# Count matrices of a graph kernel: bins added up in two strips in SBUF, each strip written once

## The reference, cut to what matters

```python
x, src, dst, edge_attr_64, edge_type_100 = inputs          # (3125,128), (103125,), (103125,), (103125,64), (103125,)
# layer 0: messages over edges with edge features
h = leaky_relu(concat([x[dst], edge_attr_64], axis=1) @ msg_w1 + msg_b1)
aggregated = segment_sum(h @ msg_w2 + msg_b2, src, num_segments=3125)
# layer 1: attention over edges; layer 2 and 3: normalised and plain mean of neighbours
alpha = exp(e - m[dst]) / denom[dst];  coef = rel_table[edge_type_100, 0] * alpha
out = segment_sum(coef[:, None] * z[src], dst, num_segments=3125)
```

## Time and profile before

| | us |
|---|---|
| median of three runs | 3433.16 |
| lowest, highest | 3431.87, 3433.22 |
| span of the profiled execution | 3432.5 |
| mean granted TensorE clock, share of full | 0.868 |
| DVE busy | 2686.0 (78%) |
| PE busy | 2529.2 (74%) |
| POOL busy | 1979.1 (58%) |
| ACT busy | 1648.7 (48%) |

### The profile page before, as it was taken

The page is one execution under the profiler, slowest core; times in us unless marked ns, Lnnn a source line. Parts: engine busy times, 40 slices in busy tenths (PEclk is TensorE's granted clock), DMA queues, the critical chain, the costliest instruction groups (busy, mean ns, idle before and its releaser), DMA issues. The chain is left out here.

```text
span 3432.5 us, 87712 instructions
## 1 busy us (share of the span) xinstructions
PE 2529.2 (74%) x20390; PEld 1959.9 (57%) x20391; DVE 2686.0 (78%) x8325; ACT 1648.7 (48%) x4130; POOL 1979.1 (58%) x2344
## 2 busy tenths in 40 slices
PE   2433555555555555999999999999999329989899
PEld 1322334443334434888888888888887214444454
DVE  8853777777777765999999999999997779993501
ACT  2011222222222224888888888888886655452200
POOL 1005777777777777888888888888887000000000
PEclk9976666677666677999999999999999559999999
DMA  9993222222222215888888888888887569868766
GB/s 382 412 414 117 79 78 78 78 78 83 78 77 78 78 63 145 230 227 229 230 227 228 231 225 228 231 227 230 228 227 244 215 284 352 300 235 304 250 218 203
DMA packets 738172, 696.85 MB, mean 203 GB/s; under 512 B 48523, under 2 KB 637274, under 8 KB 734778
## 3 DMA queue, kind: packets, MB, share of 16 engines
q1 hardware_dynamic: 516770, 536.77, 46.7%
q10 hardware_dynamic: 195544, 104.71, 12.6%
q0 software_dynamic: 25792, 54.52, 4.8%
HBM read 340.91 MB, written 354.90 MB: 203 GB/s over the span
## 5 line engine op out<-in xcount | busy, mean ns | idle before, releaser
L855 POOL DMA_INDIRECT sorted_rows<-rows,posi x806 | 784.1, 973 | 338.9 <-issue 316.6
L1137 DVE SCALAR_TENSOR_TENSOR acc<-acc,keep,pm 128x256 f32<-128x256 f32 x1504 | 717.4, 477 | 23.0 <-issue 8.3
L964 POOL TENSOR_SCALAR ohs_e<-iota,rt 128x128 f32<-128x128 f32 x1128 | 663.6, 603 | 12.5 <-DMA rt<-sorted_rows 12.5
L1064 PE MATMUL pm<-ohw_e,ohs_e 128*128 128x128 f32 x3008 | 662.6, 302 | 0.0
L803 PE MATMUL s_peq<-sb_w1bb,eT 128*128 128x256 f32 x806 | 352.2, 531 | 397.7 <-ACT eT L658 378.8
L973 POOL TENSOR_TENSOR hid<-pre_e,excess 128x512 f32<-128x512 f32 x376 | 511.8, 1361 | 141.6 <-ACT excess L1000 141.6
L1070 PE MATMUL px<-PN,dT 128*128 x4512 | 498.3, 219 | 0.1
L1016 ACT ACTIVATE ohw_e<-ohd_e,rt 128x128 f32<-128x128 bf16 x1504 | 474.6, 386 | 0.0
L1064 PEld LDWEIGHTS pm<-ohw_e,ohs_e 128*128 128x128 f32 x3008 | 459.4, 193 | 0.0
L803 PEld LDWEIGHTS s_peq<-sb_w1bb,eT 128*128 128x128 f32 x806 | 172.6, 264 | 439.4 <-ACT eT L658 431.1
L1081 PE MATMUL ps<-hid,ohs_e 128*128 128x129 f32 x3008 | 417.9, 281 | 1.2 <-POOL hid L973 1.1
(11 more groups left out here) (317 smaller groups left out, 4275.0 us busy)
## 6 DMA issues: line engine op xcount, KB each, us to landing
count_matrices<-acc SPq DMA_DIRECT2D x1504, 128.0 KB, 2.4
sorted_rows<-zrow SPq DMA_DIRECT2D x188, 528.0 KB, 10.1
rt<-sorted_rows ACTq DMA_DIRECT2D x184, 528.0 KB, 4.5
gab<-count_matrices SPq DMA_DIRECT2D x60, 1280.0 KB, 6.0
arb<-count_matrices SPq DMA_DIRECT2D x25, 1664.0 KB, 9.0
ab<-count_matrices SPq DMA_DIRECT2D x25, 1600.0 KB, 9.0
arb<-count_matrices SPq DMA_DIRECT2D x25, 1536.0 KB, 8.4
ef<-in_edge_attr_dram SPq DMA_DIRECT2D x58, 364.0 KB
```

The costliest lines, as they stand in the source:

```text
L855: pool.indirect_dma_start(sortd, bass.IndirectOffsetOnAxis(ap=posi[:, h, c:c + 1], axis=0), rows[:, h, c, :], None).then_inc(s_sc[h], 16)
L964: last = nc.gpsimd.tensor_scalar(ohs[:, k % BUFS, j, :], iota128[:], rt[:, k, j, D + 1:D + 2], None, ALU.is_equal)
L1064: last = nc.tensor.matmul(pm[:, q, j % 2, P:2 * P], ohs[:, kp % BUFS, j, :], ohw[:, kp % BUFS, j, :], start=True, stop=True)
L1137: nc.vector.scalar_tensor_tensor(acc[:, k % SUMS, j, :], before, keep[:, at:at + 1] if isinstance(at, int) else keep[:, ds(at, 1)], pm[:, ...
```

## The change

`acc`, `keep` and the table's row numbers go. In their place DVE holds two strips of 25 bins each in SBUF (`strips`, 128 x 2 x 51 x 128: two matrices, two slots of 25 columns of 128, and a blank column of zeros). A collect adds `pm` to the strip's column of its bin, or, for the first tile of a bin, to the blank column, and writes it into the bin's column. Which column is read and which is written stands in the table, and is loaded into registers: eight values a group and, by a load of its own with a check of its bounds, the strip's number, from which a wait on the writes (`s_w`) is computed. SP waits in each of 25 steps until `s_acc` has reached the tile count at which a strip ends (`ends`), and writes the strip in one transfer of 128 x 2 x 3200 numbers (3.28 MB). `ohw` and `dT` move into the space of `H`, which isn't in use in this stage. The operation of the collect is `tensor_tensor` in place of `scalar_tensor_tensor`. In the first stage one of three counting loops goes, and the transfer of `keep` to all partitions.

```diff
+SLOTS2 = 2
+BLANK = SLOTS2 * NT
-        tilei = msb("tilei", [1, 3, TT], I32)
-        keep = msb("keep", [P, TT])
+        tilei = msb("tilei", [2, 2, TT], I32)
+        ends = msb("ends", [1, NT], I32)
...
+                    nc.vector.tensor_copy(ends[:], incb[0:1, :].rearrange("p (s d) -> p s d", d=NT)[:, :, NT - 1])
-                    for k in range(3):
+                    for k in range(2):
                         for j in range(TCOL):
                             ins = nc.vector.tensor_scalar(junk4[:, j % 4, :], incb[:], kidx[:, k, j:j + 1], None, ALU.is_le,
                                                           ALU.add, accum_out=table[:, k, j:j + 1])
...
-                    act.dma_start(keep[:], tilef[0:TT].partition_broadcast(P)).then_inc(s_tl, 16)
-                    for k in range(3):
-                        act.dma_start(tilei[:, k, :], tiler[k:k + 1, 0:TT]).then_inc(s_tl, 16)
+                    for k in range(2):
+                        act.dma_start(tilei[k:k + 1, :, :], tiler[2 * k:2 * k + 2, 0:TT].unsqueeze(0)).then_inc(s_tl, 16)
...
-            acc = sb("acc", [P, SUMS, G, 2 * P])
+            strips = sb("strips", [P, 2, BLANK + 1, P])
...
             @block.sync
             def _(sp):
-                def step(i, k):
-                    n = i * RING + k
-                    rows = loads(nc, mybir.EngineType.SP, tilei[0:1, 2, ds(n * G, G)], DUMMY + SUMS * G - 1)
-                    for j in range(G):
-                        sp.wait_ge(s_acc, n * G + j + 1)
-                        sp.dma_start(ar[:, ds(rows[j], P, NT), :].rearrange("a p c -> p a c"),
-                                     acc[:, k % SUMS, j, :].rearrange("p (a c) -> p a c", a=2)).then_inc(s_w[k % SUMS], 16)
+                for s in range(NT):
+                    o = s % SLOTS2 * NT
+                    done = sp.value_load(ends[0:1, s:s + 1], min_val=1, max_val=TT)
+                    if s:
+                        sp.wait_ge(s_w, 16 * s + 32)
+                    sp.wait_ge(s_acc, done)
+                    sp.dma_start(strip[s], strips[:, :, o:o + NT, :].rearrange("p a q c -> p a (q c)")).then_inc(s_w, 16)
...
-                nc.vector.memset(acc[:], 0.0)
+                nc.vector.memset(strips[:, :, BLANK:BLANK + 1, :], 0.0)
+                nc.vector.memset(strips[:, :, 0:1, :], 0.0)
...
-                def collect(i, k, first, j):
+                def collect(i, k, first, j, at):
                     n = i * RING + k
                     if j % 2 == 0:
                         dve.wait_ge(s_m, 2 * n + j // 2 + 1)
-                    if j == 0 and not (first and k < SUMS):
-                        dve.wait_ge(s_w[k % SUMS], (i * (RING // SUMS) + k // SUMS) * (16 * G))
                     if not (first and k < 1 and j < 1):
                         dve.wait_ge(s_acc, n * G + j)
-                    nc.vector.scalar_tensor_tensor(acc[:, k % SUMS, j, :], before,
-                                                   keep[:, at:at + 1] if isinstance(at, int) else keep[:, ds(at, 1)],
-                                                   pm[:, j // 2, j % 2, :], ALU.mult, ALU.add).then_inc(s_acc, 1)
+                    nc.vector.tensor_tensor(strips[:, :, ds(at[j], 1), :].squeeze(2), strips[:, :, ds(at[G + j], 1), :].squeeze(2),
+                                            pm[:, j // 2, j % 2, :].rearrange("p (a c) -> p a c", a=2), ALU.add).then_inc(s_acc, 1)
+
+                def columns(i, k):
+
+                    n = i * RING + k
+                    at = loads(nc, mybir.EngineType.DVE, tilei[0:1, :, ds(n * G, G)], BLANK)
+                    dve.wait_ge(s_w, dve.value_load(tilei[1:2, 1, ds(n * G, 1)], min_val=0, max_val=NT) * 16 + 16)
+                    return at
...
                     if two:
-                        collect(*back(i, k, 2), first, 0)
+                        at = columns(*back(i, k, 2))
+                        collect(*back(i, k, 2), first, 0, at)
```

66 lines of the change are left out of this document (30 added, 36 removed).

## The result

The changed kernel takes **3839.45 us** (median of 4 runs, 3838.31 to 3847.43) against 3433.19 us for the kernel before, measured beside it: a ratio of 1.118, 95% interval 1.117 to 1.119. It was forecast as slower and is, but by 406 us where 180 were forecast, and outside the range of 3540 to 3720. One of the four runs beside it of the kernel before took 4389.77 us, far from the other three, and is left out of the ratio. The profiled execution has a span of 3836.3 us.

A forecast was written before the change was run, and what follows sets the result against it. Bound: a circle through PE and DVE, 3.476 us a group. Forecast: 3.97 against 3.476 times 376, +186, edges -6: 3432.5 + 186 - 6 = 3612.5, plus 0.7 for median against span: 3613 us; range 3540 to 3720.

The forecast's parts named there:

- Step (1): Collect's arithmetic on DVE: 415 ns for 256 elements against 477, all four collects shorter by 0.06 us.
- Step (3): Rest of the group after the first collect: third collect at 3.91 us, group 3.97 with the loop turn, +186 us.
- the loop turn: Branch and registers once a turn of eight groups, no longer hidden by DVE's work: 0.5 us a turn, 0.06 a group.
- Step (5): Edges outside the loop: transfer of `keep` -1.9, clearing -1.7, end -2.2, together -6 us.
- Rival D: PE's clock falls in the loop because PE is less busy; half speed adds 1070 us; chance 2%.
- step (2): DVE's sequencer work between `sums` and first collect: uncovered new piece of 1.55 us, first collect at 2.39 instead of 1.61.
- rival B: DVE's load price goes by values: 75 ns each, eight take 0.60, +89 us, 3702; 12%, 4% for a higher price.
- step (4): SP's 25 strip writes replacing 1504 waits and writes: put at nothing, 198 us as the bound.
- Rival C: Strip bursts delay the edge rows, stopping DVE up to 7.9 us each: up to 198 us more, 3811; chance 5%.
- A: DVE's loads are hidden and the circle through PE and DVE gets shorter: 3380 us; chance 8%.

The follow-up runs named there:

- x13: Changed kernel with every collect on a fixed column and no register load left in the loop, strip writes kept, sums not the reference's: 3354 us, ratio 0.976.
- x2: Changed kernel with all 25 strip writes moved after the last tile, count matrices wrong: 4002 us, ratio 1.166, loop 1642 us.
- x10: Changed kernel without the bounds check of the strip's number: 3763 us, ratio 1.097.
- x12: Changed kernel with eight columns and strip number as one load of nine neighbours, unchecked, number also used for the sums: 3638 us, ratio 1.060.
- x11: Changed kernel with every collect on column 1 by constants, no column loads or strip wait, writes reading the other slot, sums not the reference's: 3428 us.
- x5: Changed kernel with columns, strip number and wait a step earlier, between one-hots and fourth collect, in seven groups of eight: 3883 us, ratio 1.132.
- x15: Kernel before with a two-input addition as collect, its source buffer picked by a register, target constant, each tile still written separately: 3417 us, ratio 0.995.
- x4: Kernel before with a plain addition as collect and the keep left out, sums not the reference's: 3368 us, ratio 0.981.
- x1: Kernel before with a one-value load, its check and an always open wait added ahead of the first collect: 3528 us, ratio 1.028.
- x7: Kernel before with destination one-hots and source one-hot changing places in DVE's step: 3563 us, ratio 1.038.
- x8: Kernel before with the swap of x7 and the strip numbers of eight groups loaded at once, once a turn: 3663 us, ratio 1.068.

## Why the prediction was right and wrong, point by point

**Right.** The direction, and the place: one gap ahead of the first collect, `add` no longer waiting for `px` (0.2 us in 1200), hardly a pause of DVE on the strips (8.7 us in five places are put down to them). Step (1), the collect: 0.415 forecast, 0.418 measured. Step (3): first to third collect 1.52 us forecast, 1.55 in the timeline; the loop turn 0.5 us forecast, 0.51 measured. Step (5): -6 forecast, -8 measured (by the medians).

**Rival D, in part.** Its sign, a granted clock under 1.0 in the loop, did appear: the mean is 0.97, with 21 short stretches, 99 us in all, at the lower level (1.2 GHz, a granted 0.50). Each comes 6 to 12 us behind a write's issue, after a pause of PE of 1.9 to 2.7 us; the one in the window of 0.83 begins at 1515.0, behind a pause of 1.94 us that ended at 1514.66. Under the same writes without loads (x13) the clock is 1.00 throughout the loop, so the dip follows the pause and not the write. Its cost doesn't show: a matmul of `px` took 314 ns in the dips and 219 outside, but groups that lie wholly in one, with no write under way, took 4.31 to 4.37 us like the rest (4.85 where they begin a turn). The price of 1070 us was also summed wrongly: 6.70 less 3.97, times 376, is 1026.

**Wrong, first: step (2), the sequencer chain.** x2, without the strips in the loop, gives 1642 - 1298 = 344 us for steps (1) to (3), where 186 were forecast. Third to first collect was forecast at 2.39 us and takes 2.76 (1999.23 to 2001.99). The load of eight took 0.64 instead of 0.364, +0.28 us: over 376 groups 104 us. The extra price of a value had been drawn between one value on DVE and four on PE; both are one four, so the line through them said nothing of a second. The upper bound that I had written beside it, 75 ns a value and 0.60, was the right one, and so was rival B's mechanism in size if not in its rule. The check had been put at 40 ns; with its assertion it takes 213, and x10 gained 76 us without it. The two together are 0.28 + 0.17 = 0.45 us a group, 169 us, against a shortfall of 344 - 186 = 158. That sum is of rows. As runs, x10 took the check out alone; none took out the second four of columns alone, but x12, which loads nine neighbours at once and checks nothing, came to 3638 us.

**Wrong, second: step (4), the strip writes, put at nothing.** They cost 70 us (x2). The term had been looked for in the edge rows' landing and in a wait of DVE on the writes, and neither is there. x11 and x13 show the way it took instead: a strip's transfer stretches the register loads about threefold for some 8 us, and DVE's and PE's order waits behind these loads. Rival C was nearest in amount (half of it would have been 99) and had the wrong mechanism.

158 + 70, less the 2 us that step (5) gained more than forecast, is the miss of 226 us.

**The rivals.** A fell: the chain was not covered where it stands, and x5 shows that one instruction of 0.68 us doesn't cover it elsewhere. The point from which A decides was put at 0.5 us of new work and lies lower: a load of four with its registers (x15, 0.42 us and the steps between) already cost 0.11 us a group against x4, and a load with check and wait (x1) 0.19. The range's upper end, 3720, had room for B or for part of C, but not for both at once, and both came.

**In my own expectations** the worst were x7, 130 us above its upper theory, and x8, 85 us above the upper end of its second theory as counted from x7: in one the wait of a moved instruction was forgotten, in the other a price from neighbours was used for values that are apart.

## What to carry to other kernels

A register picked from a table is no free index: count what the engine's sequencer must do between two instructions of its engine, load by load, and ask what covers it; what is left over is paid in every turn. Keep the values that are loaded together side by side and at most four, leave bounds checks out of uncovered spots, and expect such loads to be three times dearer while a transfer of megabytes leaves SBUF. Take of a change the half that shortens the path (x15, 0.5% here) and leave the half that thins out a resource nobody waited for. Before an instruction is moved, move its waits in thought first.

## What the runs showed of the hardware that I had not expected

- Register loads on DVE: 0.31 to 0.32 us for one value, 0.34 for four neighbours, 0.60 for eight, 0.84 for nine, 2.15 for eight values 16 bytes apart.
- The same loads from about 1 to 8 us behind the issue of a write of 3.28 MB out of SBUF: mostly 0.9 to 1.6 us instead of 0.31 to 0.33, on DVE and PE alike. Without loads (x13) the loop ran at 3.23 us a group under the same writes.
- A bounds check behind a load: one register instruction of 190 ns and an assertion of 23, where others take 40 to 105.
- A gap that the profile gives to the last semaphore (`PE pm`, 302 of 384 us) can be mostly the sequencer's own work: in the group shown, 0.90 of the 1.22 us lie behind the end of that product. The rows of the sequencer tell.
